# Routed experts without a combine stage, and attention in one-bank units

## The reference

```python
# attention, for each image
q = einsum('oc,bcn->bno', Wq, xc);  k = einsum('oc,bcn->bon', Wk, xc)
attn = softmax(q @ k, axis=-1)
attn = attn / (1e-6 + attn.sum(axis=1, keepdims=True))
x_r = xc @ attn
t = Wt @ (xc - x_r) + bt
out = xc + relu(batchnorm(t))            # t_tokens += out

# routed feed-forward: 8 experts, hidden width 512, capacity C = ceil(1.25 * T / 8) = 1960
logits = x @ gate_w + gate_b;  probs = softmax(logits)
idx = argmax(probs);  prb = probs[idx]
pos = position of the token among the tokens of its expert;  kept = pos < C
ybuf = relu(buf @ w1 + b1) @ w2 + b2     # buf: (8, C, 128), the kept tokens
y_tok = ybuf[idx, min(pos, C - 1)] * (prb * kept)
y = nan_to_num(y_tok, nan=0, posinf=1e4, neginf=-1e4)     # t_tokens += y
```

## Time and profile before

| | us |
|---|---|
| median of three runs (lowest, highest) | 4024.82 (4021.76, 4025.27) |
| the profiled execution | 4029.11 |
| its span | 4027.3 |
| PE, PEld, DVE, ACT, POOL busy | 3220.5, 1828.0, 2844.5, 1511.0, 749.0 |
| deformable sampling's matmuls (L781) | 1379.6 |
| averages (L1589), energies (L1577, both products) | 607.1, 400.6 |
| maxima (L1774), exponentials (L1686) | 385.5, 364.9 |

### The profile page before, as it was taken

How to read it: one execution, slowest core, us unless ns; L and a number is a source line. 1 busy time by engine, 2 the same in 40 slices (tenths; PEclk the granted TensorE clock), 3 DMA queues, 4 the chain that set the end, 5 groups by cost and what they waited for, 6 DMA issues and landing times. The chain is left out here.

```text
span 4027.3 us, 40402 instructions
## 1 busy us (share of the span) xinstructions
PE 3220.5 (80%) x11501; PEld 1828.0 (45%) x11501; DVE 2844.5 (71%) x4212; ACT 1511.0 (38%) x2817; POOL 749.0 (19%) x825
## 2 busy tenths in 40 slices
PE   5998099999999999999674799899899975029930
PEld 3554055555555555555442344444445445016620
DVE  4888399999999999999596666776666635100036
ACT  2454234334333433340353564464553502013322
POOL 1545000000000000000595011111011112530046
PEclk9999599999999999999786899999999975569975
DMA  3577422111221221110523000100101012012223
GB/s 79 135 178 170 79 35 35 25 25 27 34 29 25 33 30 25 25 25 0 156 66 93 0 1 0 49 1 16 33 1 30 4 31 60 15 47 79 78 65 85
DMA packets 211450, 193.96 MB, mean 48 GB/s; under 512 B 66861, under 2 KB 182461, under 8 KB 210880
## 3 DMA queue, kind: packets, MB, share of 16 engines
q1 hardware_dynamic: 188160, 175.13, 19.9%
q0 software_dynamic: 6272, 8.99, 1.1%
q10 hardware_dynamic: 16896, 8.39, 0.7%
HBM read 94.01 MB, written 102.30 MB: 49 GB/s over the span
## 5 line engine op out<-in xcount | busy, mean ns | idle before, releaser
L781 PE MATMUL deform_acc<-deform_prod,all_ident 128*128 128x392 f32 x4096 | 1379.6, 495 | 78.4 <-DVE deform_prod L866 72.9
L781 PEld LDWEIGHTS deform_acc<-deform_prod,all_ident 128*128 128x128 f32 x4096 | 769.2, 190 | 684.3 <-DVE deform_prod L866 177.9
L866 DVE TENSOR_TENSOR deform_prod<-deform_xw,deform_wd 128x1568 f32<-128x1568 f32 x512 | 911.8, 1792 | 19.4 <-DVE deform_wd L826 11.3
L1589 PE MATMUL attn_ps_r<-attn_prob,attn_xs 128*128 128x448 f32 (+1 forms) x1400 | 607.1, 563 | 64.4 <-DVE attn_xr L1805 57.0
L1686 ACT ACTIVATE attn_prob<-attn_ps_e,attn_nm 128x896 f32<-128x896 f32 (+3 forms) x400 | 364.9, 913 | 464.9 <-DVE attn_nm L1774 463.0
L1774 DVE TENSOR_REDUCE attn_nm<-attn_ps_e 128x1 f32<-128x896 f32 (+3 forms) x400 | 385.5, 971 | 161.6 <-PE attn_ps_e L1577 150.8
L1589 PEld LDWEIGHTS attn_ps_r<-attn_prob,attn_xs 128*128 128x128 f32 (+1 forms) x1400 | 256.2, 194 | 314.4 <-issue 188.2
L745 ACT ACTIVATE deform_wd<-deform_zeros 128x3136 f32<-128x3136 f32 x32 | 90.1, 2816 | 808.5 <-DVE deform_prod L866 808.5
L2236 DVE TENSOR_TENSOR experts_yo<-experts_ps_y,experts_b 128x512 f32<-128x512 f32 x32 | 22.1, 692 | 393.1 <-PE experts_ps_y L2176 393.1
L1036 POOL MEMSET rows_half<- 128x4 f32 x1 | 0.1, 101 | 1527.3 <-POOLq L67 1527.3
L1805 DVE TENSOR_TENSOR attn_xr<-attn_xr,attn_ps_r 128x448 f32<-128x448 f32 x252 | 155.8, 618 | 160.2 <-PE attn_ps_r L1589 157.6
(11 more groups left out here) (322 smaller groups left out, 3925.3 us busy)
## 6 DMA issues: line engine op xcount, KB each, us to landing
offsets_masks<-offs_om SPq DMA_DIRECT2D x56, 378.0 KB
deform_om<-offsets_masks SPq DMA_DIRECT2D x256, 82.7 KB
deform_xw<-projected SPq DMA_DIRECT2D x256, 73.5 KB
projected<-offs_zero SPq DMA_DIRECT2D x13, 680.0 KB
dispatched<-rows_zero SPq DMA_DIRECT2D x1, 8192.0 KB
experts_bi<-dispatched SPq DMA_DIRECT2D x32, 256.0 KB, 3.4
expert_out<-experts_yo ACTq DMA_DIRECT2D x32, 256.0 KB, 3.8
projected<-offs_zero SPq DMA_DIRECT2D x15, 544.0 KB
```

What stands on the lines that cost most here:

```text
L781: mm = pe.matmul(out, ident[:, :], prod[:, s % NPROD, i, :], start=False, stop=(s == NCHUNK - 1 and i == NXH - 1))
L866: nc.vector.tensor_tensor(prod[:, s % NPROD, :, :].rearrange("p d (y x c) -> p d y x c", y=BY, x=UX), x, spread(w.rearrange("p (d y x) -> ...
L1589: mm = pe.matmul(ps_r[:, 0:BK], xs[0:rows, at + i, j // 2, :], prob[0:rows, at + i, j * BK:(j + 1) * BK], start=(i == 0), stop=(i == len(t ...
```

## The change

- Attention: `NCH` is 7, so each unit is one bank and an image has 175 units. `NE` is 5 single banks, and `ps_r` has two banks used in turn, so that an average waits for the addition before last. Due times are written in the new units. `tin` has two buffers. The first and last image's shared steps use two of the banks each in place of three. The stage writes its tokens into `out` itself; `attended` is gone.
- Routing: a row is now `ROW` = 258 numbers: the normed token, the token itself, its number plus one, and the reciprocal of its softmax sum. The scatter writes whole rows of 1032 B. `dispatched` grows to 16.9 MB, and the clearing with it.
- Experts: batches are loaded with each partition's four rows contiguous (4128 B), in eight buffers. PE's order is hidden(n), turn(n + 1), result(n - 1). After the bias ACT scales with the row's own factor, DVE does what the combine did (now 512 wide) and adds the token, and POOL scatters the finished rows into `out` by four indirect DMAs a batch (128 in all). Empty slots have number 0, which is turned into an address out of bounds. Dropped tokens keep what attention wrote. The hardware loops are written out.
- The combine stage, its 98 gathers and `expert_out` are gone.

```diff
-NCH = 4
+NCH = 7
-NE = 3
+NE = 5
...
-        at = begin(S - 1) + 1 if S else -8
+        at = begin(S - 1) + 2 if S else -8
...
-            at, lag = ((b - 1) * UNITS + 52 + 6 * g, 2) if b else (-60 + 4 * g, 5)
+            at, lag = ((b - 1) * UNITS + 91 + 10.5 * g, 3.5) if b else (-60 + 4 * g, 5)
...
-            at, lag = (base + 18 + 4 * g, 2) if b + 1 < B else (base + 18 + 2 * g, 1)
+            at, lag = (base + 32 + 7 * g, 3.5) if b + 1 < B else (base + 32 + 2 * g, 1)
...
-        NTIN = 3
+        NTIN = 2
...
-        ps_e = [t.ps(f"ps_e{i}", [128, 2, 512]) for i in range(NE)]
-        ps_r = t.ps("ps_r", [128, 512])
+        ps_e = [t.ps(f"ps_e{i}", [128, 512]) for i in range(NE)]
+        ps_r = [t.ps(f"ps_r{i}", [128, 512]) for i in range(2)]
...
-                    if n:
-                        pe.wait_ge(r_ok, n)
+                    if n >= 2:
+                        pe.wait_ge(r_ok, n - 1)
...
+ROW = 2 * C + 2
...
                     pool.indirect_dma_start(
-                        out=buf_d, out_offset=bass.IndirectOffsetOnAxis(ap=slots[:, 0, f:f + 1], axis=0),
-                        in_=hall[:, f, :], in_offset=None, bounds_check=E8 * SLOTS - 1, oob_is_err=False)\
+                        out=buf_d, out_offset=bass.IndirectOffsetOnAxis(ap=slots[:, f:f + 1], axis=0),
+                        in_=rows[:, f, :], in_offset=None, bounds_check=E8 * SLOTS - 1, oob_is_err=False)\
...
+                do(nc.vector.tensor_copy(rows[:, :, 2 * C], token[:, :]))
...
+                dve.wait_ge(sm_ok, 2)
+                do(nc.vector.tensor_reduce(sm[:, :], ex[:, :, :], AX, ALU.add))
+                do(nc.vector.reciprocal(rows[:, :, 2 * C + 1], sm[:, :]))
                 dve.wait_ge(tri_ps, 1)
...
-        bufv = buf_d.rearrange("(b i p) c -> b p i c", p=128, i=NI)
+        bufv = buf_d.rearrange("(b p i) c -> b p i c", p=128, i=NI)
...
+                def rows(n):
+                    if n >= NBI:
+                        sp.wait_ge(fin, n - NBI + 1)
+                    sp.dma_start(bi[:, n % NBI, :, :], bufv[n]).then_inc(bi_in[n % NBI], 16)
...
+                turn(0)
+                for n in range(NBT + 1):
+                    if n < NBT:
+                        hidden(n)
+                    if n + 1 < NBT:
+                        turn(n + 1)
+                    if n:
+                        result(n - 1)
...
+                def scale(n):
+                    p = n % 2
+                    if n >= NFX:
+                        act.wait_ge(y_st[n % NFX], 64 * (n // NFX))
+                    nc.scalar.activation(fx[:, n % NFX, :, :], zeros[:, :, :], ACT.Copy).then_inc(blank, 1)
+                    act.wait_ge(y_ok, n + 1)
+                    if n >= 2:
+                        act.wait_ge(fin, n - 1)
+                    for j in range(NI):
+                        last = nc.scalar.activation(yc[:, p, j, :], yo[:, p, j, :], ACT.Copy,
+                                                    scale=bi[:, n % NBI, j, 2 * C + 1:ROW])
+                    last.then_inc(scaled, 1)
...
+                def finish(n):
+                    p, f = n % 2, n % NFX
+                    dve.wait_ge(scaled, n + 1)
+                    y = yc[:, p, :, :]
+                    do(nc.vector.tensor_tensor(mk[:, 0, :, :], y, y, ALU.is_equal))
...
+                    nc.vector.tensor_tensor(fx[:, f, :, :], bi[:, n % NBI, :, C:2 * C], fx[:, f, :, :], ALU.add)\
+                        .then_inc(fin, 1)
+
+                for n in range(NBT + 1):
+                    if n < NBT:
+                        add_bias(n)
+                        row_numbers(n)
+                    if n:
+                        finish(n - 1)
...
+                for n in range(NBT):
+                    p = n % NFX
+                    pool.wait_ge(row_ok, n + 1)
+                    pool.wait_ge(fin, n + 1)
+                    for j in range(NI):
                         pool.indirect_dma_start(
+                            out=out, out_offset=bass.IndirectOffsetOnAxis(ap=row_i[:, p, j:j + 1], axis=0),
+                            in_=fx[:, p, j, :], in_offset=None, bounds_check=T - 1, oob_is_err=False).then_inc(y_st[p], 16)
```

More of the change, by code:

```diff
@@ L1574, in energy @@
                     for q_, k_ in ((qa, ka), (qb, kb)):
[L1575 to L1578 removed]
+                        mm = pe.matmul(ps_e[u % NE][0:rows, 0:BK], q_[:, S % 2, at:at + rows],
+                                       k_[:, b % 2, ch * BK:(ch + 1) * BK], start=q_ is qa, stop=q_ is qb)
                     mm.then_inc(e_ps, 1)
@@ L2180, in _, with hidden @@
-                turn(0, 0)
-                with pe.Fori(0, E8 // 2 - 1) as i:
-                    pair(i, False)
-                pair(E8 // 2 - 1, True)
+                def hidden(n):
+                    e = n // NEB
+                    if n % NEB == 0:
+                        pe.wait_ge(w_in[e % 2], 32 * (e // 2 + 1))
+                    pe.wait_ge(bt_ok, n + 1)
+                    for f in range(FB):
+                        if n:
+                            pe.wait_ge(hid_ok, (n - 1) * FB + f + 1)
+                        pe.matmul(ps_u[f][:, :], w1[:, e % 2, f * 128:(f + 1) * 128], bt_[:, n % 2, :], start=True,
+                                  stop=True).then_inc(u_ps, 1)
@@ L2191, in _ @@
                 act.wait_ge(b1_ok, 1)
-                def turned(n, p):
-                    hold(act, bT, n + 3, own)
-                    nc.scalar.activation(bt_[:, p, :], ps_t[p][:, :], ACT.Copy).then_inc(bt_ok, 1)
-                def store(n, p):
-                    hold(act, y_ok, n + 3, own)
-                    act.dma_start(resv[n], yo[:, p, :, :]).then_inc(y_st[p], 16)
-                def pair(i, first, last):
-                    for at in range(2 * NEB):
-                        n, e, p = i * (2 * NEB) + at, i * 2 + at // NEB, at % 2
-                        for f in range(FB):
-                            hold(act, u_ps, n * FB + (f + 1), own)
-                            nc.scalar.activation(hid[:, p, f, :], ps_u[f][:, :], ACT.Relu,
-                                                 bias=b1t[:, bass.ds(e * FB + f, 1)], scale=1.0).then_inc(hid_ok, 1)
-                        if not (last and at == 2 * NEB - 1):
-                            turned(n + 1, 1 - p)
-                        if not (first and at == 0):
-                            store(n - 1, 1 - p)
@@ L2213, in _, with turned @@
-                turned(0, 0)
-                pair(0, True, False)
-                with act.Fori(1, E8 // 2 - 1) as i:
-                    pair(i, False, False)
-                pair(E8 // 2 - 1, False, True)
-                store(E8 * NEB - 1, 1)
-                for p in range(2):
-                    act.wait_ge(y_st[p], 16 * E8 * NEB // 2 + 1)
+                act.wait_ge(cst, 3)
+                def turned(n):
+                    act.wait_ge(bT, n + 1)
+                    if n >= 2:
+                        act.wait_ge(u_ps, (n - 1) * FB)
+                    nc.scalar.activation(bt_[:, n % 2, :], ps_t[n % 2][:, :], ACT.Copy).then_inc(bt_ok, 1)
@@ L2240, in combine_stage @@
-def combine_stage(nc, k, res_d, tok, slots, weight, out):
-    own = k["own"]
-    with ExitStack() as es:
-        t = Ctx(nc, es, "combine")
-        yg = t.sb("yg", [128, 2, FG, C])
-        yc = t.sb("yc", [128, 2, FG, C])
-        fx = t.sb("fx", [128, 2, FG, C])
-        mk = t.sb("mk", [128, 3, FG, C], I32)
-        lim = t.sb("lim", [128, 2, FG, C])
-        step, res, cst, scaled = (t.sem(s) for s in ("step", "result_ready", "constants_ready", "rows_scaled"))
-        zeros = t.sb("zeros", [128, FG, C])
-        got = [t.sem(f"gathered{p}") for p in range(2)]
-        stored = t.sem("stored")
-        outv = out.rearrange("(p f) c -> p f c", p=128)
-        with nc.Block() as block:
+                count = [0]
@@ L2330, with ffn @@
+                for p in range(NFX):
+                    pool.wait_ge(y_st[p], 64 * NBT // NFX)
+def ffn(nc, k, c, ins, buf_d, out):
+    route_stage(nc, k, ins, out, buf_d)
+    experts_stage(nc, k, ins, buf_d, out)
 _NAMES = ["x", "L0_conv_w_in", "L0_conv_b_in", "L0_conv_w_dw", "L0_conv_b_dw", "L0_conv_ln_dw_g", "L0_conv_ln_dw_b",
```

300 lines of the change are left out of this document (133 added, 167 removed).

## The result

| | us |
|---|---|
| before, measured again beside it: median of four (lowest, highest) | 4024.72 (4021.76, 4025.27) |
| after: median of four (lowest, highest) | 3815.82 (3811.91, 3818.66) |
| ratio (95% interval) | 0.9482 (0.9465 to 0.9498) |
| the profiled execution of after, its span | 3811.91, 3809.8 |

The change takes 209 us off; the prediction said 230, with a range that holds the result. The first thing to do with such a result is to split it at the stages' borders, in the two traces. The border is the first DMA that SP issues for the next stage, or the first exponential for attention.

A forecast was written before the change was run, and what follows sets the result against it. PE bounds attention, though not fully, and the experts' stage; POOL's gathers bound the combine. Experts and combine -174.1, routing +1.3, attention -57 make -230: median 3795 us, range 3718 to 3860 (likeliest case 3745 to 3845).

The forecast's parts named there:

- the room: Attention's main part: 1011 us minus a floor of PE work leaves 116 to 132 us to win, 125 used.
- the term for `xs`: Attention: PE waits some 3 us for POOL's longer `xs` after three-tile sub-blocks, 20 times: 60 us lost, bounds 0 and 100.
- the 8 us of hand-overs: Attention: another 8 us of the room lost to hand-overs around key steps.
- The maxima: Attention: column maxima go from 400 to 700, adding 45 us to DVE (38 by the skill), total time unmoved.
- The stage's end: End of attention: 5 us won from waits of averages against 7 lost to two `tin` buffers; together 0, bounds -10 and +8.
- Routing: Routing stage: a few more DVE operations cost +1.3 us; scatter price taken as unchanged.
- Rival C: Scatters: 1032 B rows cost double on POOL, +96 us, 3891 us in all; chance 0.05.
- The period of a batch: Experts' stage: the new PE order cuts a batch from 8.36 to 7.53 us, 31 x 0.83 = 26 us, other engines hidden.
- Rival D: Experts' stage: DVE work delays POOL's scatters to 1.92 us, +44, 3839 us; chance 0.04, of it 0.03 for slower than before.
- Start and tail: Experts and combine: combine goes, rows load 1.5 us earlier, 15.8 us from last result to end; -174.1 us with the batch gain.
- A: Attention: PE saturated, `xs` not late, the whole 125 us won, 3727 us; chance 0.14.
- B: Attention gains nothing, as `xs` costs 5 us each time and DVE bursts use up the cover: 3852 us; chance 0.16.

The follow-up runs named there:

- e3: The changed kernel with one bank for the averages and six, not five, for the energy units: 3846.55 us, ratio 0.9563.
- e4: The changed kernel with averages due 6.5 units behind each sub-block's end except the stage's last two (4.5 behind three-tile ones before): 3784.87 us, ratio 0.9411.
- e8: The changed kernel with averages due 8.5 units behind a sub-block's end (less for the last four), plus the tail and start edits of e7: 3778.42 us, ratio 0.9395.
- e2: The changed kernel's attention stage with routing, experts and combine of the kernel before: 3981.08 us, ratio 0.9888.
- e7: The changed kernel, with DVE finishing each of the last six batches right behind its bias and PE's first turn not waiting for the output bias: 3802.76 us, ratio 0.9461.
- e9: The kernel e8 with averages due 6.5 units behind a sub-block's end as in e4, tail and start as in e7: 3775.31 us, ratio 0.9386.
- e1: The changed kernel's routing and experts, without combine, with the attention stage of the kernel before: 3860.12 us, ratio 0.9596.
- e5: The changed kernel with PE's old order in the experts' stage, hidden(n), turn(n + 1), result(n): 3832.74 us, ratio 0.9529.

## Why the prediction was right, and where its steps were off

**Attention: the room was counted as one sum.** The prediction subtracted a floor of work from the stretch, called the rest (125 us) the room, and let the second bank win all of it but what `xs` and key steps would take. What became of it can be read from the starts of all matmuls of the stretch. A step from one start to the next is usually 0.376 us for an average and 0.189 for an energy; what is over that is put down to the pair of matmuls between which it lies (us, each rounded, from the first to the last matmul between the first and the last exponential):

| | before | one bank (e3) | after | lag 6.5 (e4) | lag 8.5 (e8) |
|---|---|---|---|---|---|
| averages and energies at their usual steps | 772 | 774 | 774 | 774 | 774 |
| steps from the smaller matmuls | 101 | 102 | 102 | 105 | 112 |
| over, energy to average | 76 | 59 | 32 | 20 | 5 |
| over, average to average | 23 | 24 | 24 | 14 | 10 |
| over, all other pairs | 36 | 35 | 45 | 35 | 51 |
| sum | 1008 | 993 | 977 | 947 | 951 |

Only the third row is what a wait ahead of a block of averages costs: 76 us in before. The forecast's room held 23 us inside blocks of averages and 36 elsewhere as well, which the second bank did not take away. So the step that failed is the room, 125 where 76 stood to be won; the term for `xs`, 60, was too large as well (32 us are left in that row, and the profile's own rows give it 28.5 to 34.5), and the 8 us of hand-overs came to 8 in the last row. 76 - 32 - 8 is some 35, and 4 of it are lost in the other rows: 31, where the stretch between the exponentials is 32 shorter. A room 49 us too large stood against a wait some 28 too large, and 57 came out for 32. Nor was it the second bank alone that took the third row down: 76 to 59 came with the one-bank units (and a sixth bank for them), 59 to 32 with the bank.

For `xs` the durations were right (1690 ns for an operation over seven chunks, forecast 5.3 / 3 = 1.77 us), and so was the ranking: it is late next. It happened 11 to 15 times and not 20, and for 2.3 to 2.6 us in the mean, not 3. From the last energy of a three-tile sub-block to the end of its `xs` the trace has 8.5 us in the median, forecast 8.7 to 9.8. In the cases without a wait PE came later than its 5.9 us of work allow; what held it up there was not followed. The table also shows why e4 gave more than its row for `xs`: 12 us came from there (32 to 20), 10 from the inside of blocks (24 to 14) and 9 from the other pairs, and 2 went to the smaller matmuls. Where in PE's order the averages fall also decides what the blocks next to them cost; why the inside of a block is cheaper there is not settled.

**The maxima** are 700 now, with 407.2 us busy in all, 22 more than the 385.5 of the 400 before. The forecast was 45 more, from 619 ns alone; three in a row take 1.68 us, so 0.56 each. The overhead of the Trainium skill (Perfetto Trace Analysis, Optimizing Scalar/DVE Operations), some 125 ns for a DVE operation on PSUM, gave an estimate of 38 us. It was right in its sign and too large here. The section recommends larger operations for a saturated engine, which DVE, busy for 707 of 978 us, is not; the total did not suffer by the split.

**The stage's end** was put at nothing, bounds -10 and +8, and gave 15, outside them. The failed term is that for the waits of averages, "5 us, and up to 10 more if the clock holds", of which the forecast took the 5. The last averages in before, and below them in after:

```profile
3274.11 3.65 PE L1589 MATMUL attn_ps_r<-attn_prob,attn_xs 128*128 128x448 f32 x4 [0.71 <-DVE attn_xr L1805]
3278.48 3.65 PE L1589 MATMUL attn_ps_r<-attn_prob,attn_xs 128*128 128x448 f32 x4 [0.71 <-DVE attn_xr L1805]
```

```profile
3212.51 13.34 PE L1584 MATMUL attn_ps_r<-attn_prob,attn_xs 128*128 128x448 f32 x28 [0.42 <-POOL attn_xs L1486]
```

In before each block of averages waits 0.71 us or more for the addition, and behind four such blocks the granted clock falls from 1.00 to 0.50 (1.2 GHz) at 3256.6; the last six blocks, of four matmuls each, take 3.65 us apiece. In after the last seven blocks run without a wait between them, 13.34 / 7 = 1.91 us apiece, and the clock falls only at 3228.0, when they are done. With one average bank (e3) it falls at 3249.8, and only the last two are slow (3.39 and 3.65 us). From the last exponential to the last average there are 37.9 us in before, 28.9 in e3 and 19.2 in after: 19 us won, some 8 from waits and 10 from the clock (six blocks, 1.74 us each). What the prediction allowed as "up to 10 more" came whole. Against it stand the two `tin` buffers, forecast at 7 us: from the first finished group of tokens to routing's first DMA there are 24.7 us in after and 19.7 in before, 5 more (23.6 to 24.7 in e2, e3, e4, e7 and e9 as well, all with two buffers, and 19.1 in e1 with three; no run changes the buffers alone). So that term was about right, and the total of nothing came from leaving the clock's part out.

**Routing** is 0.1 us shorter, forecast +1.3; e1 and e3, with the same stage, have 268.2 and 269.1 where after has 265.9, so a term of this size can't be told. Rival C, a double price of the longer rows, is refuted with 976 ns.

**The period of a batch**: 7.45, forecast 7.53 and 7.5 to 7.7. Here all terms were spans of PE read off one batch, with nothing else late, and the cover was summed engine by engine: DVE 65%, forecast 5.5 of 7.5; ACT 60, forecast 73; POOL 49, or 63 with the gaps of 0.30 us behind its 115 scatters, forecast 76. The new order gave 19 us by e5, forecast 26; the period itself came out because another 0.3 us a batch went too, for which the prediction had no term. That part was luck.

**Rival D**, DVE holding up POOL's descriptor work: the mean is 1051 ns against 976 alone, and no scatter of after has more than 1.26 us, where D reckoned with 1.92. Nor is it any work of DVE that does it. The 28 scatters of after that run beside the bias addition and the small row-number operations have 972 ns; the 28 beside the comparisons (L2282 to L2284) and the first predicated copy (L2287) have 1058, and the 29 beside the predicated copies alone (L2287, L2289) have 1179. The Trainium skill (SBUF — State Buffer, Who interferes with whom) also makes it depend on the kind of DVE operation; that the shared port is what holds these scatters no run here shows. The growth from 620 to 3100 ns of its other section is not in this trace, which has 8% in the mean.

**Start and tail**, -174.1 forecast, -165.4 measured. The period came out 0.08 x 31 = 2.5 better; against it the start was 9.6 us and not 6.7 (the first transposition waits for the semaphore of two biases, and the larger one, issued fourth behind it, holds PE until 7.5 us after its issue); and the tail was 24.2 and not 15.8. The sum of that tail followed one batch alone. Its steps were sized well: finishing took 4.6 us, forecast 4.3, a scatter with its gap 1.28, forecast 1.3. What was left out, and is the step that failed here, was the queue ahead of the last batch. PE makes the last two results back to back, since there is nothing hidden left to put between; DVE's order has the finishing a batch behind the bias. So two finishings (3788.78 to 3797.9) and not one, and on POOL six scatters left from 3797.5 on and not four. e7 took that lag off and won 4.6 us of the 8.4.

**Rivals A and B**: A (PE saturated, 3727) is refuted by 34.5 us of waits for `xs`; B (attention gains nothing) by e2, -45 us. The forecast held because both halves' mechanisms were right, and because its errors stood against each other: attention 25 us too much, the experts' stage 9 too much, the stage's end 15 too little. Of the signs named beforehand, those of the missing combine stage, the wait for the addition near 0, the period and route's scatters came as said. The attention stretch (977 us) and the 34.5 us of `xs` waits fell just outside their bands of 940 to 970 and 40 to 90, the tail well outside 15 to 17, and "waits of energies for the exponentials over 30 us" (45.4) would have called the prediction wrong: that sign was ill chosen, since at these loads the matmuls' steps are only 9.6 us over their usual length.

## What to carry to other kernels

When a wait is to be removed, count as its price only the idle time that lies in front of the waiting instruction; stretch minus floor also holds spacing that no edit of the wait touches. When work is moved behind a loop with a lag, walk through the last two iterations on each engine in its written order, since lag and backlog come out there in full, and count how many buffers close a loop through all engines: eight against four was worth 219 us here. And look at the granted clock where waits of 0.7 us lie between short bursts of matmuls: at the end of attention the waits cost 8 us and the lower clock 10. And an order of work written with due times deserves a scan of its lag: one number gave 31 us, as much as the second bank, and its far side shows as a new wait on another engine.

## What the runs showed of the hardware

- An indirect DMA of 128 rows costs POOL 975 ns at 512 B a row and 976 ns at 1032 B, with 0.30 us between two. Beside DVE's comparisons and predicated copies on 128 x 512 float32 it has 1.06 to 1.18 us in the mean and up to 1.26 (1.35 in e7); beside a bias addition from PSUM it stays at 972 ns.
- Three column maxima of 448 over PSUM in a row take 1.68 us, though one alone has 0.61 to 0.62.
- A weight load can be shown waiting (45.4 us, 118 times) while the matmuls lose little: the steps between their starts at these places are 9.6 us over the usual ones in all. From the last average of a block to the next energy the starts are 0.37 to 0.47 us apart in 239 of 246 cases.
- At the end of attention in before, with 0.71 us idle ahead of each block of four averages and the granted clock at 0.50, a block came every 4.37 us; in after, with no such wait and the clock at 1.00, every 1.91 us.
